# One reciprocal per attention head, and the second bank of its values normalised by ScalarE instead of VectorE

## What is computed

```python
q = (x @ Wq + bq).reshape(Bsz, Tlen, NUM_HEADS, HEAD_DIM)
kv = x @ Wkv + bkv
k, v = (kv[..., :HEAD_DIM], kv[..., HEAD_DIM:])
q = q + pe[None, None, :, :]      # after a transpose to heads
k = k + pe[None, :, :]
scores = jnp.einsum('bhqd,bkd->bhqk', q, k) * scale
scores = jnp.where(causal[None, None, :, :], scores, jnp.finfo(scores.dtype).min)
probs = jax.nn.softmax(scores, axis=-1)
attn = jnp.einsum('bhqk,bkd->bhqd', probs, v)
out = jnp.transpose(attn, (0, 2, 1, 3)).reshape(Bsz, Tlen, NUM_HEADS * HEAD_DIM)
return out @ Wo
...
x = _layernorm(x + _L0_attn_ref(x, ...), axis=-1)
x = _layernorm(x + _L0_ffn_ref(x, ...), axis=-1)
```

## Time and profile before

| | |
|---|---|
| time, median of 3 runs | 1847.6 us (1845.06 to 1848.81) |
| the profiled execution's own time | 1832.81 us |
| its span, on the slowest core (core 3) | 1831.2 us |
| spans of the 8 cores | 1809.7 to 1831.2 us |
| PE busy | 1562.0 us, 85% |
| DVE busy | 1142.5 us, 62% |
| ACT busy | 988.0 us, 54% |

### The profile page before, as it was taken

How to read it: one execution, slowest core, us unless ns; L and a number is a source line. 1 busy time by engine, 2 the same in 40 slices (tenths; PEclk the granted TensorE clock), 3 DMA queues, 4 the chain that set the end, 5 groups by cost and what they waited for, 6 DMA issues and landing times.

```text
span 1831.2 us, 36386 instructions; the slowest of 8 cores (1809.7 to 1831.2 us)
## 1 busy us (share of the span) xinstructions
PE 1562.0 (85%) x15296; PEld 830.7 (45%) x15296; DVE 1142.5 (62%) x2300; ACT 988.0 (54%) x1417; POOL 522.9 (29%) x907
## 2 busy tenths in 40 slices
PE   4699999989988989889997998989997999777633
PEld 2355666534644545434553644533553556323200
DVE  1456544687654665887654574788555566777745
ACT  3445657467765636356774834447674757146500
POOL 1143140302103062721303053540301224730046
PEclk9899999999999999999999999999999999988855
DMA  8999882435557498943737598964556669868997
GB/s 255 194 156 138 147 157 46 119 122 152 197 154 243 163 279 291 286 167 121 221 139 213 180 261 288 273 218 156 148 179 185 221 205 354 281 242 292 342 284 301
DMA packets 120965, 383.18 MB, mean 209 GB/s; under 512 B 10000, under 2 KB 29488, under 8 KB 107616
## 3 DMA queue, kind: packets, MB, share of 16 engines
q1 hardware_dynamic: 84096, 282.10, 47.4%
q0 software_dynamic: 36560, 97.70, 22.7%
q10 hardware_dynamic: 144, 1.05, 0.2%
HBM read 281.19 MB, written 148.90 MB: 235 GB/s over the span
## 4 chain that ended last, share of the span: by engine, by line
PE 63%; DMA 18%; DVE 11%; ACT 4%; POOL 2%; issue 2%; SPq 1%; POOLq 0%; DVEq 0%; ACTq 0%
PE X L520 12%; PE X L417 10%; PE S L492 10%; PE X L595 9%; PE X L735 7%; DMA xTb<-xT 5%; DMA rp_scratch<-rpn 4%; PE X L853 3%; DMA rpe<-rp_scratch 3%; PE S L759 3%; DVE pTn L539 3%; DMA xT<-xT 2%; PE X L442 2%; ACT pr L499 2%; PE X L454 2%
## 5 line engine op out<-in xcount | busy, mean ns | idle before, releaser
L499 ACT ACTIVATE pr<-S 128x1024 bf16<-128x1024 f32 (+2 forms) x640 | 564.1, 903 | 330.7 <-PE S L492 324.3
L520 PE MATMUL X<-vS,pr 128*128 128x129 bf16 x4352 | 363.3, 220 | 24.8 <-DVE pTn L539 23.0
L520 PEld LDWEIGHTS X<-vS,pr 128*128 128x128 bf16 x4352 | 285.8, 98 | 146.3 <-DVE pTn L539 53.2
L492 PE MATMUL S<-qT,kT 128*128 128x512 bf16 (+3 forms) x1280 | 341.7, 348 | 7.9 <-DVE e1tmp L785 5.4
L404 ACT CAST rpn<-X 128x512 bf16<-128x512 f32 x280 | 162.4, 591 | 152.0 <-PE X L853 117.9
L595 PE MATMUL X<-w_o,atT 128*128 128x512 bf16 x992 | 235.2, 385 | 9.6 <-ACT rpn L404 6.9
L417 PE MATMUL X<-xTb,w_q 128*128 128x512 bf16 x864 | 204.5, 383 | 5.9 <-ACT atT L404 1.6
L404 ACT CAST gq<-X 128x512 bf16<-128x512 f32 x270 | 153.5, 589 | 91.1 <-PE X L735 71.3
L405 DVE CAST gq<-X 128x512 bf16<-128x512 f32 x242 | 164.3, 690 | 29.7 <-PE S L759 10.7
L424 DVE SCALAR_TENSOR_TENSOR qT<-X,bq_s,pe_s 128x512 bf16<-128x512 f32 x116 | 86.9, 749 | 119.2 <-PE X L417 119.1
L853 PE MATMUL X<-w2s,inr 128*128 128x512 bf16 x384 | 135.7, 381 | 28.2 <-DVE xw L602 10.6
(11 more groups left out here) (137 smaller groups left out, 1948.2 us busy)
## 6 DMA issues: line engine op xcount, KB each, us to landing
rp_scratch<-rpn SPq DMA_DIRECT2D x128, 512.0 KB, 5.6
rpe<-rp_scratch SPq DMA_DIRECT2D x56, 1024.0 KB, 11.8
xw<-x SPq DMA_DIRECT2D x64, 512.0 KB, 6.2
w1s<-cw SPq DMA_DIRECT2D x32, 1024.0 KB, 5.6
x_scratch<-xw POOLq DMA_DIRECT2D x60, 512.0 KB, 6.9
x2f<-x_scratch SPq DMA_DIRECT2D x52, 512.0 KB, 8.0
y<-x2f POOLq DMA_DIRECT2D x52, 512.0 KB, 8.9
w2s<-cw SPq DMA_DIRECT2D x48, 512.0 KB, 4.7
```

Of the source, the lines that this page charges most:

```text
L492: t = P.pe(lambda e, kc=kc, q0=q0, col=col, w=w, slot=slot: e.matmul(S[sl][:, col: col + w], kT[slot][:, (kc % 4) * 128: (kc % 4) * 128 + ...
L499: ex = P.act(lambda e: e.activation(out=pr[pl][:, 0: width], in_=S[sl][:, 0: width], func=AF.Exp, bias=-CSHIFT, scale=SCALE), [pr_free[pl] ...
L520: t = P.pe(lambda e, kc=kc, q0=q0, col=col, sub=sub, c0=c0, slot=slot: e.matmul(PV[sub // 2][:, c0: c0 + 129], pr[pl][:, col + sub * 128 - ...
```

## The change

In `emit_norm` one reciprocal now takes all four sums of the head (the buffers `rc` grow from two to four floats, and there are still two of them, used in turn). DVE normalises bank 4 with one product, as before. ACT normalises bank 5 with two scaled copies of 128 columns, the scale being read from `rc`. Bank 4 is free after DVE's product and bank 5 after ACT's second copy, and the transposes wait for both. The costs given to the planner are 0.17 and 0.45 us on DVE and 0.31 us for each copy on ACT, in place of 0.17 + 0.45 + 0.17 + 0.45 us on DVE.

```diff
-    rc = [sb(f"rc{i}", 2, F32) for i in range(2)]
+    rc = [sb(f"rc{i}", 4, F32) for i in range(2)]
...
-        for hb in range(2):
-            ra = P.dve(lambda e, hb=hb: e.reciprocal(rc[hb], view(PV[hb], 128, (132, 2))), [rc_free[hb], t],
-                       cost=0.17)
-            rc_free[hb] = P.dve(lambda e, hb=hb: e.tensor_tensor(
-                view(pTn[slot], hb * 256, (128, 2), (1, 128)), view(PV[hb], 0, (132, 2), (1, 128)),
-                view(rc[hb], 0, (1, 2), (0, 128)), ALU.mult), [ptn_free[slot], ra], cost=0.45)
-            free[4 + hb] = rc_free[hb]
-        ptn_tok[(n, h)] = (slot, rc_free[1])
+        i = k % 2
+        ra = P.dve(lambda e: e.reciprocal(rc[i], view(X, 128, (512, 2), (132, 2))), [rc_free[i], t], cost=0.17)
+        free[4] = P.dve(lambda e: e.tensor_tensor(
+            view(pTn[slot], 0, (128, 2), (1, 128)), view(PV[0], 0, (132, 2), (1, 128)),
+            view(rc[i], 0, (1, 2), (0, 128)), ALU.mult), [ptn_free[slot], ra], cost=0.45)
+        for j in range(2):
+            free[5] = P.act(lambda e, j=j: e.activation(
+                out=pTn[slot][:, 256 + j * 128: 384 + j * 128], in_=PV[1][:, j * 132: j * 132 + 128], func=AF.Copy,
+                scale=rc[i][:, 2 + j: 3 + j]), [ptn_free[slot], ra], cost=0.31)
+        rc_free[i] = free[5]
+        ptn_tok[(n, h)] = (slot, [free[4], free[5]])
...
-                [const_tok["ident"], free[b], tok], done=(sub == 3))
+                [const_tok["ident"], free[b]] + tok, done=(sub == 3))
```

More of the change, by code:

```diff
@@ L535, in emit_norm @@
         assert k < 3 or ptn_free[slot] is not None
-        for hb in range(2):
-            ra = P.dve(lambda e, hb=hb: e.reciprocal(rc[hb], view(PV[hb], 128, (132, 2))), [rc_free[hb], t],
-                       cost=0.17)
-            rc_free[hb] = P.dve(lambda e, hb=hb: e.tensor_tensor(
-                view(pTn[slot], hb * 256, (128, 2), (1, 128)), view(PV[hb], 0, (132, 2), (1, 128)),
-                view(rc[hb], 0, (1, 2), (0, 128)), ALU.mult), [ptn_free[slot], ra], cost=0.45)
-            free[4 + hb] = rc_free[hb]
-        ptn_tok[(n, h)] = (slot, rc_free[1])
+        i = k % 2
[9 more added lines that the diff above has]
+        ptn_tok[(n, h)] = (slot, [free[4], free[5]])
         ptn_free[slot] = None
-        chain["T"].append(Unit(0.0, lambda: n == 0 or (n - 1) in at_free, lambda: [ptn_tok[(n, h)][1]],
+        chain["T"].append(Unit(0.0, lambda: n == 0 or (n - 1) in at_free, lambda: ptn_tok[(n, h)][1],
                                lambda: unit_t(n, h)))
```

## The result

The changed kernel took **1857.6 us** (median of 5 runs, 1855.92 to 1859.53) where the kernel before took 1847.7 in the same comparison: a ratio of 1.0051, with a 95% interval of 1.0034 to 1.0067. That is slower by 10 us, 6 to 12. The forecast was 1854, slower, in a range of 1842 to 1866.

A forecast was written before the change was run, and what follows sets the result against it. PE's stream was taken to bound the kernel. Bank 5 on ACT +8.6, ACT's copies waiting for DVE +1, DVE's shorter queue -4 and the new order elsewhere +1 gave +6.6 on 1847.6: 1854.2 us, range 1842 to 1866.

The forecast's parts named there:

- PE's stream bounds the kernel: Whole kernel: PE busy 1562.0 of 1831.2 us, so DVE or ACT edits count only where PE idles for them.
- Bank 5 on ACT: End of each head: ACT frees bank 5 0.25 us later, norm waits 33 us for 24.3: +8.6 us (+3.6 to +20.9).
- The new order elsewhere: Units moved by the planner, such as three scatter units behind blocks 8 and 12: +1 us (-4 to +5).
- the fuller heads: Between value steps: planner lengthened eleven short fills, alone 3 us off the norm waits (18.3 for 21.2).
- The ends of blocks 8 and 12: Three scatter units behind the last heads there lengthen that end by up to 4 us; earlier heads shorten nearly as much.
- my own sign of "wrong": Listed as showing the forecast wrong: ends of blocks 8 and 12 longer by more than 4 us.
- The copies wait for DVE, and exponentials stand behind them: ACT's queue: exponentials absorb the added 0.5 to 0.6 us, an eviction may not: +1 us (0 to +4).
- DVE's shorter queue: PE's other waits for DVE, 13.4 us, shrink by 30%: -4 us (0 to -13.4).
- The copies are dear: Rival, 17%: ACT's copies free bank 5 at the high end, +19 us, 1867; middle of the case 1862.
- DVE's queue is what holds PE: Rival, 20%: late norms come earlier and PE's other waits for DVE vanish: -10 us, 1838.
- The change isn't what it says: Rival, 1%: ACT's copies need their own table, two loads a head, 328 us more, 2176 us.

The follow-up runs named there:

- order_only: Kernel before with its old norm (four instructions on DVE), all else in the changed kernel's instruction order: 1860.9 us, ratio 1.0093.
- one_newplan: One reciprocal and both products on DVE, nothing on ACT, in the changed kernel's order: 1845.8 us, ratio 1.0012 to the kernel before.
- one_recip: Kernel before, order kept, with one reciprocal of all four sums and both products on DVE: 1834.0 us, ratio 0.9949; measured again 0.9946.
- mech_only: The change's new norm instructions (bank 5 by ACT copies) in the order of the kernel before: 1918.2 us, ratio 1.0405.
- mech_load: The change's instructions in the old order, plus a second reciprocal and product on DVE per head: ratio 1.0427 to the kernel before.
- one_recip_own_2: Repeat run: one reciprocal, both products on DVE, order planned with that shorter norm's costs, against the kernel before: 1829.4 us, ratio 0.9919.

## Why the prediction was right in its number and wrong in two steps

The sum was 8.6 + 1 - 4 + 1 = +6.6; +10 was measured. Two of its steps failed by far more than that, and other costs and gains that it didn't have made up for them. That the number came out is luck.

- **PE's stream bounds the kernel, and the norm waits go from 23 to 33 us: right in total (32.9),** but not in the bank that they belong to. ACT's `pTn` was to be named for most of them and is for 8.0. Nor are these 10 us the 10 by which the kernel is slower: PE's waits for evictions fell by 19 at the same time, all its waits together fell from 248 to 240, and its busy time grew by 11.
- **Bank 5 on ACT (+8.6): the mechanism right, the sum over heads wrong.** At the place of the earlier trace rows the bank comes 0.30 later (0.25 forecast, bounds 0.16 and 0.46), and the third matmul's idle time is 0.52 for 0.25. A scaled copy is 369 ns, the range given was 290 to 400. The trace agrees roughly with the Trainium skill ("ScalarE: Activation LUTs", "What ACT_TABLE_LOAD costs"), by which a copy of 128 columns with one pointer operand is an estimated 0.39 us with an overlap of 0.093; 0.369 and 0.10 were measured. But over all heads bank 5's wait fell from 12.9 to 8.4. The count assumed that bank 4 is read at +0.65 in every head. Where DVE is late, PE waits for bank 4, and the copies run beside bank 4's product meanwhile.
- **"The new order elsewhere" (+1, -4 to +5) and the fuller heads (-3): this step failed.** `order_only` measured +17. I had counted what the new order puts between two value steps on PE against one need, +1.15 (and bank 4 read at +0.65), taken at a head whose reciprocal begins at once. In over half of the heads of blocks 4 to 15 it begins late, 1.4 us on average in the old order and 1.0 in the new, mostly with the mask (L507) or a statistic ahead of it on DVE. The old order had enough of PE's work behind all of these heads and the new one hasn't behind 20, so bank 4's wait goes from 10.7 to 24 us. In the blocks with qb = 0, for which 2.3 us were forecast, bank 4's wait is 13.5 to 14.5 in the changed kernel (5.4 to 6.0 before). `one_newplan` against `one_recip` shows the same with other instructions. How the order's 17 us come about beyond the longer ends and the clock stays open, since other waits fell by nearly as much as these grew.
- **The ends of blocks 8 and 12 (up to 4 us longer): under-sized.** Both are 4.3 us longer or more, up to 6.4 on one core, as the three units and their waits for DVE take about the 4 us that were given, and the stretch of little work that they make is followed by PE's clock at 1.2 GHz (0.9 or 1.7 us on the router's matmuls). That was my own sign of "wrong", and it came.
- **"The copies wait for DVE, and exponentials stand behind them" (+1, 0 to +4): this step failed for the old order and was hidden in the new.** In the order of the kernel before, the ACT copies cost 75 us, and a wait of ACT alone 42. I had asked whether the exponential behind the copies could be late, and not the eviction of `atT` behind that. In the new order most of this is gone: PE's waits for evictions by ACT are 93 us in `mech_only` and 33 in the changed kernel, with 0.7 for `atT` in place of 37, and the new instructions together are worth 1.0051 against 1.0093, -8 us.
- **DVE's shorter queue (-4, 0 to -13.4): the sign not contradicted, the size open.** PE's wait for L602's sum fell from 10.6 to 5.1, those for `qT` and `rpn` rose from 2.8 and 1.7 to 4.9 and 4.8, which leaves about -0.3. The load in `mech_load` gave 4 us with overlapping intervals.
- **The rivals.** "The copies are dear" had the right size of a copy but a result 4 to 9 us too high. "DVE's queue is what holds PE" was half true: DVE's late reciprocals do hold PE, and the change's own order, in which they are late by less, leaves less of PE's work beside them. "The change isn't what it says" fell: one table load.

**The account.** Old to new order, +17. One reciprocal in place of two, -15. Bank 5 on ACT, +7. The sum of +9 is no check, since each step is the difference of two neighbouring kernels and the last is the changed one; what is measured is the price of each step in this sequence. Taken in the other sequence, with the order last, it reads -9 (`one_recip`), +84 (ACT in the old order, 1.0405 for 0.9949) and -65 (the new order). The parts aren't additive. With the norm wholly on DVE the new order costs 12 to 17 us, and with bank 5 on ACT it saves 65.

**What stays open:** how the 75 us divide between ACT's waiting and its work, beyond "both, and in blocks 8 and 12 more waiting"; most of the order's 17 us; the size of DVE's relief; and which of the planner's numbers (the cheaper DVE norm or the dearer ACT) made it take PE's work away from the heads with late reciprocals. `one_recip_own_2`, with the cheaper norm alone, doesn't have the long ends of blocks 8 and 12, which points at ACT's costs, but no run changed those alone.

## What to carry to other kernels

When a planner sets the order, freeze it and measure the edit and the order apart: here the same instructions were +4.1% in one order and +0.5% in another, and the order alone was +0.9%. Before a step is moved to another in-order engine, ask what it will wait for there and list everything queued behind it down to the first thing PE needs; a copy of 0.2 us that waited for another engine's result cost 2.3%. Don't take the growth of one wait for the growth of the time before the sum of all waits and the busy time say so: here the norm waits grew by 14 us by the order, and all waits by 3. And take a change of two halves apart: the single reciprocal was the gain (0.9919 with its own order), the second engine was the loss.

## What the hardware showed that I had not expected

**Cores in pairs.** The spans of the eight cores of the changed kernel, with their granted clock:

```profile
core 0: 1848.3 us, clock 0.941
core 1: 1814.6 us, clock 0.944
core 2: 1858.0 us, clock 0.936
```

Cores 0 and 1, 2 and 3 and so on end 33 to 40 us apart here. Over ten executions of the kernel before in these comparisons the earlier of a pair ended at 1810.2 on average and the later at 1835.2, and either could be the later. The execution profiled ahead of the prediction was one of small gaps, 7.7 to 21.5 us, which fits its lying 15 us below the median. The gap opens in blocks 7 and 11 and behind block 15: block 7 took 122.4 us on the quickest core of the changed kernel and 133.5 on the slowest. On core 2 the share of the transfer engines is 1.04 and 1.00 in the middle of block 7 (655 to 675 and 675 to 695 us) and 0.93 from 1700 us to the end. The metric is that of the later cores, so a gain that only the earlier cores see doesn't count. I didn't test what the two share.

**A clock that a new order can lose.** PE's busy share of 5.1 in 9 us behind block 8 was followed by a granted clock of 0.50, and four matmuls of 512 columns went from 1.04 to 1.89 us. In the kernel before, PE was busy for 4.04 of 6 us at that place and kept 1.00.
